# Four stacked image blocks: biases of channel attention in a free channel direction, first image's queries stacked in two sets, folds behind the down-sampling

## The reference, cut to what matters

```python
x = x + L0(_gn(x))   # attention, 8 heads of 32; keys/values from a 2x2 stride-2 convolution, layer norm over channels
x = x + L1(_gn(x))   # gated scan over pixels in four directions, depthwise 3x3 convolution
x = x + L2(_gn(x))   # channel attention: layer norm per pixel, q, k, v; softmax(q k^T) over 32 channels of a head
x = x + L3(_gn(x))   # per-channel mix of max pools 1, 3, ... 13, the window chosen by a score
```

## Time and profile before

| | us |
|---|---|
| median of 3 runs | 767.22 (766.24 to 768.68) |
| the profiled execution | 768.66 |
| its span, first to last instruction | 766.9 |
| TensorE busy in it | 661.2 |
| VectorE busy in it | 556.1 |
| ScalarE busy in it | 419.2 |
| GpSimd busy in it | 35.7 |

### The profile page before, as it was taken

The page is one execution under the profiler, slowest core; times in us unless marked ns, Lnnn a source line. Parts: engine busy times, 40 slices in busy tenths (PEclk is TensorE's granted clock), DMA queues, the critical chain, the costliest instruction groups (busy, mean ns, idle before and its releaser), DMA issues.

```text
span 766.9 us, 9383 instructions
## 1 busy us (share of the span) xinstructions
PE 661.2 (86%) x3384; PEld 315.2 (41%) x3384; DVE 556.1 (73%) x1057; ACT 419.2 (55%) x703; POOL 35.7 (5%) x27
## 2 busy tenths in 40 slices
PE   4947998898999989999999897999579769799777
PEld 3633533343233354443534543343225324455332
DVE  3366347624646586854999798987898997998597
ACT  0304454759588488556776765575649565322321
POOL 3300000100002000000020000000210000000000
PEclk9967998899999999999999799999769969899979
DMA  7350123001000240001002200003000001000101
GB/s 263 97 151 2 56 48 111 2 1 56 1 1 0 48 112 2 2 1 56 0 1 48 56 2 2 1 1 110 1 1 1 0 1 56 0 1 0 56 1 55
DMA packets 15663, 26.87 MB, mean 35 GB/s; under 512 B 3409, under 2 KB 7153, under 8 KB 15490
## 3 DMA queue, kind: packets, MB, share of 16 engines
q1 hardware_dynamic: 12320, 22.80, 9.8%
q10 hardware_dynamic: 3298, 3.48, 1.6%
HBM read 14.09 MB, written 4.19 MB: 24 GB/s over the span
## 4 chain that ended last, share of the span: by engine, by line
PE 56%; DVE 19%; ACT 14%; issue 3%; DMA 3%; SPq 3%; ACTq 1%; DVEq 0%
PE PSB L1654 8%; PE PSB L1782 7%; PE PSB L1763 7%; PE PSB L1688 4%; PE PSB L1796 4%; PE PSB L1885 4%; PE PSB L1828 3%; PE PSB L1728 3%; ACT PT L631 3%; PE PSB L1748 3%; SPq L485 2%; DVE NEGMAX L1160 2%; DVE HB L1490 2%; PE PSB L1675 2%; PE PSB L2053 2%
## 5 line engine op out<-in xcount | busy, mean ns | idle before, releaser
L1160 DVE TENSOR_REDUCE NEGMAX<-PSB 128x2 f32<-128x512 f32 x128 | 80.4, 680 | 45.6 <-PE PSB L1728 45.5
L631 ACT ACTIVATE PT<-PSB 128x512 f32<-128x512 f32 x128 | 67.9, 604 | 64.8 <-PE PSB L1748 64.3
L1782 PE MATMUL PSB<-XNP,WTAP 64*64 64x512 f32 x576 | 64.5, 599 | 1.9 <-DVE XR L1203 1.9
L1728 PE MATMUL PSB<-KST,QST 96*128 96x256 f16 x256 | 44.1, 324 | 10.0 <-DMA KST<-KL 6.9
L1748 PE MATMUL PSB<-QST,KST 98*128 98x512 f16 x128 | 39.5, 413 | 10.2 <-DMA QST<-ML 7.2
L963 POOL TENSOR_TENSOR GA<-GA,PT 128x1024 f32<-128x1024 f32 x8 | 20.1, 2525 | 503.2 <-ACT PT L659 503.2
L1728 PEld LDWEIGHTS PSB<-KST,QST 96*128 96x128 f16 x256 | 26.7, 114 | 32.8 <-DMA KST<-KL 8.5
L1495 DVE TENSOR_TENSOR PA_<-HB 128x1024 f32<-128x1024 f32 x32 | 39.2, 1225 | 0.7
L1763 PE MATMUL PSB<-PT,VT 128*32 128x512 f32 x256 | 34.5, 610 | 5.9 <-ACT PT L631 4.6
L1782 PEld LDWEIGHTS PSB<-XNP,WTAP 64*64 64x64 f32 x576 | 22.2, 135 | 41.9 <-issue 41.8
L695 ACT ACTIVATE U<-PSB 64x512 f32<-64x512 f32 x32 | 26.6, 831 | 22.6 <-PE PSB L1782 22.0
(11 more groups left out here) (299 smaller groups left out, 1349.3 us busy)
## 6 DMA issues: line engine op xcount, KB each, us to landing
XF<-in_x SPq DMA_DIRECT2D x8, 512.0 KB, 3.8
QST<-QH SPq DMA_DIRECT2D x32, 128.0 KB, 2.4
XR<-in_x SPq DMA_DIRECT2D x4, 1024.0 KB, 5.0
QST<-QL SPq DMA_DIRECT2D x16, 128.0 KB, 3.0
out<-ACC SPq DMA_DIRECT2D x2, 1024.0 KB, 6.2
out<-ACC SPq DMA_DIRECT2D x8, 256.0 KB, 2.1
PS<-in_cw ACTq DMA_DIRECT2D x1, 1152.0 KB
WDS<-in_wds SPq DMA_DIRECT2D x1, 1024.0 KB, 7.1
```

What stands on the lines that cost most here:

```text
L631: e.activation(PROB[:, 4 * kt + j, :], bank("A", b, f"st{g}_{kt}_{j}")[:, :], ACT.Exp)\
L1160: e.tensor_reduce(NEGMAX[:, h, 2 * j:2 * j + 2], bank("A", b, f"s{h}_{j}")[:, :].rearrange("p (t k) -> p t k", t=2), AX.X, ALU.max, negate ...
L1728: mm = e.matmul(s[:, t * NK:(t + 1) * NK], QST[0:96, h, qt * P:(qt + 1) * P], KST[0:96, h, :], start=True, stop=True)
L1782: mm = e.matmul(banks[gi][64 * half:64 * half + 64, :], WTAP[rows, cc, tap(2 * cc + gi, dy, dx), :], XNP[rows, cc, dy + 16 * half:dy + 16 ...
```

## The change

In channel attention, each normed pixel gets -1 added in all channels (in the bias PBI of its normalisation, one VectorE operation more). As its channels otherwise sum to zero, the constant direction is free: W2Q and W2K are changed once, by subtracting the mean over input channels and bias/256 (`centred_weights` on TensorE, two subtractions on VectorE), so that products with the shifted pixels hold the biases. The ones column, the `rows` step, `srow` and the one-row matmuls of T1 and A go. The Gram matrix is symmetric: the second block is computed for its last 128 columns only, and its first 128 are a transpose of the first block (`gramT`), which waits for VectorE's copy of that block.

In the first image, the queries of heads 0 to 3 are stacked when the first 128 channels' queries are split, before the keys, and those of heads 4 to 7 after the keys, in copies of half the size with their own semaphores. The loads of the next images become a stream X of SyncE. TensorE's fold stands behind the down-sampling, and VectorE's key and value part of `setup` between the split of the first queries and the key norm. VectorE no longer waits for GpSimd's memset at its start. In `pool_score`, four pairs of operations become single ones with broadcast operands, or two steps one, five instructions fewer an image. All order strings and all bank tables are new.

```diff
@@ orders
-F4 A3 F4 A3 F4 A3 F3 A3 M6
+F5 X1 A3 X1 F3 A3 F2 X1 F1 A3 F3 A2 M1 A1 M5
...
@@ PE_ORDER, beginning
-F11 A35 F1 A6 F1 A1 F1 A3 F1 A2 F1 A27 F2 C1 F1 C4 A10 C1 A5 C1 A1 F1 A23 F1 B1 C2 A1 B1 A3 B1 A1 B1
+F11 A20 F1 A25 F1 A2 F1 A12 F1 A13 F1 A2 F2 C4 F1 C1 F1 A9 C1 A5 C1 A6 F1 A20 B1 C2 B1 A2 B1 A1 B1
...
@@ SyncE
+            def first_queries(m, ready, landed):
+                def copy(quad, j, src):
+                    sp.dma_start(QST[32 * quad:32 * quad + 32, 4 * m + j, :], src[32 * j:32 * j + 32, m, :]).then_inc(landed[j], 16)
+                sp.wait_ge(*act_f.at(0, ready[0]))
+                for j in range(4):
+                    for quad in (0, 2):
+                        copy(quad, j, QH)
+                yield
+                sp.wait_ge(*dve_f.at(0, ready[1]))
+                for j in range(4):
+                    copy(1, j, QL)
+                yield
...
+                    yield from first_queries(0, ("qh0_1", "ql0_1"), stacked)
                 sp.wait_ge(*act_f.at(b, "kh1"))
...
+                if b == 0:
+                    yield from first_queries(1, ("qh1_0", "ql1_0"), high_stacked)
...
-            interleave("SP", {"F": images(stream_f), "A": images(stream_a), "M": images(store)}, SP_ORDER)
+            interleave("SP", {"F": images(stream_f), "X": images(load, 1), "A": images(stream_a), "M": images(store)}, SP_ORDER)
@@ VectorE
-                e.memset(XNT[:, :, C:C + 1], 1.0).then_inc(*dve_d.step("xnt_ones"))
...
+                e.tensor_scalar(PBI[:, :], PBI[:, :], -0.5, -1.0, ALU.mult, ALU.add).then_inc(*dve_d.step("pbi"))
...
-                e.wait_ge(*pe_d.at(b, "rows"))
-                e.tensor_copy(SROW, bank("D", b, "rows")[0:1, 0:2 * C]).then_inc(*dve_d.step("srow"))
...
-                for cc in range(CC):
-                    e.tensor_scalar(CGE[:, cc, :], KIDX[:, :], SC[:, cc:cc + 1], None, ALU.is_le).then_inc(*dve.step(f"cge{cc}"))
+                e.tensor_tensor(CGE[:, :, :], KIDX[:, :].unsqueeze(1).broadcast_to([P, CC, KPOOL + 1]),
+                                SC[:, :].unsqueeze(2).broadcast_to([P, CC, KPOOL + 1]), ALU.is_le).then_inc(*dve.step("cge"))
...
+                if b == 0:
+                    setup_keys()
+                    yield
                 yield from kv_norm(b)
...
+                e.wait_ge(*pe_cen.at(0, "centre"))
+                for n, (w, label) in enumerate(((W2Q, "w2q"), (W2K, "w2k"))):
+                    off = bank("N", 0, "centre")[:, n * C:(n + 1) * C].unsqueeze(1).broadcast_to([P, CC, C])
+                    e.tensor_tensor(w[:, :, :], w[:, :, :], off, ALU.subtract).then_inc(*dve_cen.step(label))
...
-            e.wait_ge(*pool_set.at(0, "hb"))
@@ TensorE
+            def centred_weights():
+                s = take("N", 0, "centre", dve_cen, "w2k")
+                e.wait_ge(late_loaded, 16 * LATE_N)
+                for n, w in enumerate((W2Q, W2K)):
+                    at = slice(n * C, (n + 1) * C)
+                    for cc in range(CC):
+                        e.matmul(s[:, at], mat("mean256"), w[:, cc, :], start=(cc == 0), stop=False)
+                    mm = e.matmul(s[:, at], mat("mean256")[64:65, :], ROWS[:, at], start=False, stop=True)
+                mm.then_inc(*pe_cen.step("centre"))
...
-                        mm = e.matmul(s[:, 0:C + 1], XNT[:, t, m * P:(m + 1) * P], XNT[:, t, :],
+                        mm = e.matmul(s[:, m * P:C], XNT[:, t, m * P:(m + 1) * P], XNT[:, t, m * P:C],
                                       start=(t == 0), stop=(t == QT - 1))
...
+                e.wait_ge(*dve_d.at(b, "gram0"))
+                e.transpose(bank("D", b, "gram1")[:, 0:P], GRAM[:, 0, P:C], mat("ident")).then_inc(*pe_d.step("gramT"))
...
-                s = take("D", b, "rows", dve_d, "srow")
-                for cc in range(CC):
-                    e.matmul(s[0:1, cc * P:(cc + 1) * P], GRAM[:, cc, C:C + 1], mat("ident"), start=True, stop=True)
-                for cc in range(CC):
-                    e.matmul(s[0:1, C:2 * C], GRAM[:, cc, C:C + 1], W2Q[:, cc, :], start=(cc == 0), stop=False)
...
-                    mm = e.matmul(s[:, m * C:(m + 1) * C], SROW[:, m * P:(m + 1) * P], ROWS[:, 0:C], start=False, stop=True)
...
+                yield from down(b)
                 if b == 0:
                     setup()
                     yield
-                yield from down(b)
```

More of the change, by code:

```diff
@@ L107 @@
 PE_D = """
-gn2 xnT0 xnT1 xnT2 xnT3 gram0 gram1 rows T1 A PAT WE be cst R0 R1 out_0_0 out_0_1 out_1_0 out_1_1
+gn2 xnT0 xnT1 xnT2 xnT3 gram0 gram1 gramT T1 A PAT WE be cst R0 R1 out_0_0 out_0_1 out_1_0 out_1_1
 """
@@ L541, in stream_f @@
             def stream_f(b):
-                if b:
-                    yield from load(b)
                 yield from stack(b)
@@ L1564, in stream_d @@
                 yield from channel_norm(b)
-                yield from ones_column(b)
                 yield from pixel_stats(b)
@@ L1888, in gram @@
                     yield
+                e.wait_ge(*dve_d.at(b, "gram0"))
+                e.transpose(bank("D", b, "gram1")[:, 0:P], GRAM[:, 0, P:C], mat("ident")).then_inc(*pe_d.step("gramT"))
+                yield
             def channel_scores(b):
-                s = take("D", b, "rows", dve_d, "srow")
+                s = take("D", b, "T1", act_d, "t1")
                 e.wait_ge(*dve_d.at(b, "gram1"))
-                for cc in range(CC):
-                    e.matmul(s[0:1, cc * P:(cc + 1) * P], GRAM[:, cc, C:C + 1], mat("ident"), start=True, stop=True)
-                for cc in range(CC):
-                    e.matmul(s[0:1, C:2 * C], GRAM[:, cc, C:C + 1], W2Q[:, cc, :], start=(cc == 0), stop=False)
-                e.matmul(s[0:1, C:2 * C], ROWS[:, 2 * C:2 * C + 1], ROWS[:, 0:C], start=False, stop=True)\
-                 .then_inc(*pe_d.step("rows"))
-                yield
-                s = take("D", b, "T1", act_d, "t1")
-                e.wait_ge(*dve_d.at(b, "srow"))
+                e.wait_ge(*dve_cen.at(0, "w2k"))
                 for m in range(CC):
                     for cc in range(CC):
-                        e.matmul(s[:, m * C:(m + 1) * C], GRAM[:, cc, m * P:(m + 1) * P], W2Q[:, cc, :], start=(cc == 0), stop=False)
-                    mm = e.matmul(s[:, m * C:(m + 1) * C], SROW[:, m * P:(m + 1) * P], ROWS[:, 0:C], start=False, stop=True)
+                        mm = e.matmul(s[:, m * C:(m + 1) * C], GRAM[:, cc, m * P:(m + 1) * P], W2Q[:, cc, :],
+                                      start=(cc == 0), stop=(cc == CC - 1))
                 mm.then_inc(*pe_d.step("T1"))
@@ L1914, in channel_scores @@
                     for cc in range(CC):
-                        e.matmul(s[:, m * P:(m + 1) * P], T1[:, cc, m * P:(m + 1) * P], W2K[:, cc, m * P:(m + 1) * P],
-                                 start=(cc == 0), stop=False)
-                    mm = e.matmul(s[:, m * P:(m + 1) * P], SROW[:, C + m * P:C + (m + 1) * P],
-                                  ROWS[:, C + m * P:C + (m + 1) * P], start=False, stop=True)
+                        mm = e.matmul(s[:, m * P:(m + 1) * P], T1[:, cc, m * P:(m + 1) * P], W2K[:, cc, m * P:(m + 1) * P],
+                                      start=(cc == 0), stop=(cc == CC - 1))
                 mm.then_inc(*pe_d.step("A"))
@@ L2027, in stream_d @@
             def stream_d(b):
+                if b == 0:
+                    yield from centred_weights()
                 yield from group_norm(b, 2, pe_d, dve_d, act_d)
```

181 lines of the change are left out of this document (96 added, 85 removed), and 6 rows, old and new, of the table BANKS_B.

## The result

The changed kernel takes 761.81 us (759.70 to 762.35), the kernel before beside it 767.25 us (766.24 to 768.68): a ratio of 0.9923 (95% interval 0.9898 to 0.9948), 5.4 us less. Forecast were 18.5 us less, 748.7; the range ended at 761, 0.8 us short. The profiled execution, the slowest of the four, took 762.35 us, span 760.6.

What follows compares the result with a forecast made beforehand. The bound was taken to shift by stage: TensorE around 300 and 690 us, VectorE around 610 and after 740. Terms -6.8 - 14.5 + 3.0 + 0.4 - 1.6 + 1.0 = -18.5 gave 748.7 us, range 739 to 761.

Steps and rivals of the forecast that it cites:

- Part 1, the start: Program start: first statistics near 4.3 us, down-sampling from about 11.2 for 10.2, fold 1.7, queries at 23.1 instead of 25.38.
- Part 2, the stack: Image 0's query and key copies: scores 16.2 us after the queries, at 39.3 instead of 47.5, 8.2 us earlier.
- four weight scalings of 0.34 us: VectorE ahead of image 0's key norm: moved scalings and two bias additions overlap, 1.3 us together.
- The total of -6.8: Start and stack together, after some 1.4 us of waiting for image 1's load; bounds -4.5 and -8.5.
- Rival (b): VectorE bounds from 380 us on; -13.0 at best, poorer fit of orders takes 2 to 3; about 757, chance 0.22.
- Part 3, channel attention: All images: 5.5 us less TensorE each, worth 4.5 in images 0 and 3, 2.75 in 1 and 2; -14.5.
- wait for their maximum rows anyway: Channel attention: image 2's transposed scores, queued behind the new transpose's wait of up to 1.2 us, wait regardless.
- VectorE alone sets the pace after 740 us: End of the program: a TensorE instruction saved there is worth little; no size given.
- Centring: TensorE ahead of image 0's sums: centring W2Q and W2K adds 2.96 us, no cover claimed; +3.0.
- Pool scores: VectorE: five instructions fewer, 0.85 us an image, counted for images 2 and 3; -1.6, bounds 0 and -3.4.
- The load ahead of the stack: SyncE, images 1 and 2: image loads stand before copies that scores wait for; +1.0, bounds 0 and 3.
- (d): Images 2 and 3: thinner matmul work leaves TensorE at 1.2 GHz, 24 us more; 773, slower, chance 0.07.

Runs made afterwards that it cites:

- experiment 1: Kernel before, VectorE no longer waiting at its start for GpSimd's last memset; 766.57 us, ratio 0.9982.
- experiment 2: Kernel before, its own orders, with some 5.4 us less TensorE work in the channel attention of each of images 0 to 2; 765.33 us, ratio 0.9968.
- experiment 3: Kernel before, with the 5.4 us cut of TensorE's channel-attention work in image 3 alone; 763.57 us, ratio 0.9951.
- experiment 6: Kernel before, its own orders, with only the fused pool scores, five VectorE instructions fewer an image; 765.91 us, ratio 0.9986.
- experiment 13: Kernel before, its own orders, with channel attention cut in all four images, fused pool scores and the early start, without the two-set stack; 760.08 us, ratio 0.9891.
- experiment 4: Changed kernel, VectorE taking the last four maxima of image 1's first half ahead of image 2's remaining statistics; 757.40 us, ratio 0.9868.
- experiment 5: Changed kernel, its orders kept, GpSimd's subtraction of image 0's pixel means waiting for image 1's sixteenth maximum; 757.37 us, ratio 0.9900.
- experiment 7: Changed kernel, centring of W2Q and W2K cut from six matmul groups to two, 2.2 us less TensorE; 760.32 us, ratio 0.9915.
- experiment 9: Changed kernel, its orders kept, 14.4 us of TensorE's channel-attention work put back in images 0 to 2; 767.44 us, ratio 0.9999.
- experiment 10: Changed kernel, 4.8 us of TensorE's channel-attention work put back in image 3 alone; 763.05 us, ratio 0.9940.
- kernel 8: Experiment 4's kernel, with GpSimd's scaling of the convolution taps also waiting for image 0's key norm; 753.06 us, ratio 0.9823.
- experiment 11: Kernel 8, with all four of image 2's statistics and two further steps also behind image 1's maxima on VectorE; 755.61 us, ratio 0.9829.
- experiment 12: Kernel 8, with 14 useless float32 matmuls in TensorE's waits in each of images 0 and 1; 759.21 us, ratio 0.9884.
- experiment 14: Kernel 8, with fewer useless matmuls in TensorE's waits: 5 and 3 in image 0, 3 and 4 in image 1; 754.79 us, ratio 0.9825.

## Why the prediction was wrong, point by point

**The forecast's mechanism was half of it.** The start and image 3 were right in mechanism and near in size. Between them lie two losses that the sum does not have: at image 1's maxima the new orders, which it took as neutral, give back the start's gain, and from there to image 3 the savings of images 0 to 2 bring nothing.

**Part 1, the start: right.** First statistics 4.27 us (4.3 expected), down-sampling from 11.22 (11.2) for 9.69 (10.2), fold 1.7 (1.7), queries from 22.46 (23.1). From the Trainium skill, "TensorE: Matmul & The Clock Gate", Part 1 (the clock is low by default, and activity raises it), I had worked out a down-sampling longer by up to 3.5 us without the fold in front, and a sum 1.7 us worse. It was 0.5 us shorter, and the traces show no such rise: 8.8 to 10.2 us with the fold in front (experiments 1, 2, 3, 6, 13 and the kernel before), 8.6 to 9.8 without it (the ten others).

**Part 2, the stack: right in mechanism, 2.7 us short at the scores of this trace.** From the queries to the scores I counted 16.2 us; it was 19.6. The failed step is "four weight scalings of 0.34 us" that overlap to 1.3 us together. They had been moved beside GpSimd's scaling of the taps (22.85 to 29.70 us in the changed kernel), and KB, VB and the scalings took 2.8 us from 27.56 to 30.37. TensorE waited 2.25 us for the keys and then did them at 1.2 GHz (granted clock 0.67 from 32 to 36 us), 3.56 us for 1.97. Together these are some 3 us. How much of it comes varies between executions: in the five traces with the same start (experiments 4, 5, 7, 9, 10) queries to scores take 17.2 to 17.6 us, and with the taps later (8, 11, 12, 14) 16.9 to 17.1. So 0.7 to 0.9 us of the count were missing without any collision. I had weighed what the moved steps hold up on VectorE and TensorE, and not what GpSimd runs beside them.

The Trainium skill has the rule, "SBUF — State Buffer", section "Who interferes with whom": a VectorE instruction with two inputs in SBUF contends with a GpSimd instruction that reads SBUF, one in a mode that uses two ports contends with GpSimd, whichever issues first keeping the shared ports for the whole instruction, and one with at most one SBUF input outside these modes does not. The traces agree: 1.55 and 1.71 for two inputs (0.17 alone), while L1146 with one input in PSUM keeps its 0.69, and the reductions of MV_F their 0.15. The total of -6.8 became -5.3 at the transposed scores, within its bounds; the five other traces have -6.9 to -7.9 there.

**The step that failed most: the new orders at no cost.** Rival (b) had "a poorer fit of the new orders' waits" at 2 to 3 us; the sum had nothing. At image 1's maxima the fit cost all that the start had gained: the lead of 5.5 us at image 0's sums is 0.35 at the maximum rows. In what VectorE did in front of the last four maxima, 1.3 us of statistics, 1.4 of variance and 3.3 of two small operations under GpSimd's lock, the lock is the larger half (5.2 us lost, 2.2 without the lock, 0.2 in the other order); shown is that the stall shrinks when either of the two, order or lock, is changed (experiments 4 and 5); that only the order brings the time past the normalisation is read from the two traces. The two repairs, maxima and taps, together are 8.8 us by the medians (ratio 0.9923 to 0.9823, intervals apart). That was readable in advance: the new order string of VectorE in the diff puts F's steps ahead of A's last six. I read the orders of TensorE and SyncE for what waits there, and VectorE's not.

**Part 3, channel attention: size right, worth wrong.** The saving an image is what was worked out: in image 3's chain -1.7 for Gram, +0.1, -1.9 for `rows`, -1.2 for T1, -0.8 for A, -5.5 us as predicted. Its worth for image 3, 4.5 predicted, is 3.7 of 5.4 in the old orders (experiment 3) and 4.3 of 4.8 in the trace of the new ones (experiment 10, where the medians have 1.2). For images 1 and 2, 2.75 each predicted, experiment 13's trace has 0.8 and 1.2 (the pool scores included), less than the 1.5 of rival (b). For image 0, 4.5 predicted, the same trace has a loss of 1.4. The failed step, in the old orders, is to take a full TensorE in the earlier trace rows for a bound. From 300 to 320 us it was full, but the Gram block at 290 lay inside the trip of image 2's maximum rows. I had written that the transposed scores "wait for their maximum rows anyway" and used it only to excuse a new wait; it should have struck 1.8 us of Gram off the term. Nor do say that VectorE alone sets the pace after 740 us: TensorE is at 18.3 of 20 there.

Images 0 to 2 together: 10 predicted, 2.4 measured in the old orders. In the new orders the same work does count: put back, 14.4 us of it cost 5.6 by the medians and 7 to 11 in the traces, 3.9 of 4.8 for image 0. And yet the saving brings nothing there. From image 0's convolution (150 us in the kernel before) to the sums ahead of image 3's channel attention (642) the lead over the kernel before changes by -2.3 to +1.2 us in nine traces of the new orders with the work saved, by +0.4 and +0.6 in the old orders with it cut (experiments 2 and 13), and by -9.5 in the new orders with it put back. So in the new orders the savings go into making up for the orders; through which waits is not shown.

**The small terms.** Centring, +3.0: nothing that experiment 7 can tell. "TensorE is full there" failed in the same way: what comes behind it waits for VectorE. Pool scores, -1.6: -1.1, with an uncertainty that is larger still; the trace has 1.9. The load ahead of the stack, +1.0, was not tried by itself.

**The rivals.** (b), 754 to 763, holds the measured time and names the fit of the orders, at half of what it cost; its place, VectorE from 380 us on, is wrong for the loss at 130 us and not tested for what goes behind it. (d): the granted clock fell, to 0.58 around 610 us, where VectorE has no gap to give. A price for it was found ahead of the transposed scores of images 0 and 1, where it did not reach the end (experiment 14), and behind the cut Gram block of experiment 2, 2.3 us on two groups of scores. That no other stretch pays for it was not tried.

**The books, by the two traces.** The changed kernel's lead over the kernel before is 5.3 us at image 0's transposed scores (6.8 forecast), 0.9 at image 0's convolution, 0.8 at those sums of image 3 and 6.3 at the end. So the start is 1.5 short, and that beside a slow start of the kernel before. Image 1's maxima take 4.4 that the sum does not have. From the convolution to image 3 the sum has 5.6 (10 for images 0 to 2, less 3.0, 0.4 and 1.0), and nothing comes. Behind that, 5.5 of 6.1 come (image 3 and the pool scores). Together these are the 12 us between 18.5 and 6.3.

By the times kernel 8, which has both repairs, is 14.1 us under the kernel before on its chip (767.20). Experiment 13, the savings without the early stack, has 7.8 of that; the stack's 6.1 is argued from where the scores start in the two traces (39.0 and 45.1) and not measured by itself.

**Open.** Why the work of images 0 to 2 counts for more in the new orders than in the old ones (2.4 of 16), and why the medians (5.6) and the traces (7 to 11) of experiment 9 differ, isn't settled; the changed kernel's own trace, with its slow keys, is behind the others from the start. Nor is the stretch from 625 to 665 us, where the changed kernel's lead goes from 4.8 us to -1.2 while VectorE's new order has image 2's pool windows among image 3's scan output. Of this 2.0 us go from the sums at 642 to 665 us, and the stretch behind makes 7.4 instead of the 5.5 of the matmuls, so pool work was perhaps only moved; that was not taken apart.

## What to carry to other kernels

A saving on a busy engine is worth little if the saved work stood between the start of a copy and its landing: look for the wait that follows the work before crediting it. A step that is moved takes on its neighbours on the other engines: for each small VectorE operation at its new place, look at what GpSimd runs then. And a new order string is a change by itself: walk each engine through it at the places where another engine waits for a round trip, here the last maxima ahead of the transposed scores.

## What the runs showed of the hardware

- Beside GpSimd's element-wise operations, VectorE operations of 0.15 to 0.17 us on 8 columns took 1.55 and 1.71 us, scalings of 0.34 took 1.08 and 1.15, and a normalisation of 2.34 took 4.41; the first two ended when a GpSimd instruction did. A subtraction with one input in PSUM kept its 0.69 us beside it.
- After a wait of 3.1 us the same eight transposed scores take 3.75 us, and 2.06 where useless products filled the wait to 0.6; the granted clock of the 20 us is 0.70 and 0.93.
- A float32 product of 128 x 512, which the trace holds as two instructions, took 0.88 us at the high level (fourteen instructions in 6.17).
